# The feed-forward weights of a fused attention and FP4 feed-forward layer, begun a chunk in every second step

## What is computed

```python
q = elu(x @ Wq + bq) + 1; k = elu(x @ Wk + bk) + 1; v = x @ Wv + bv
k = k / sqrt(sum(k * k) + 1e-6)
out = (q @ k.T) @ v @ Wo + bo                 # by head
x = layernorm(x + (layernorm(x + out) * gamma + beta))

def fp4_quant_dequant(x):                      # of each block of 16
    scale = max(max(abs(xb)) / 6, 1e-12)
    q = GRID[searchsorted(MID, abs(xb / scale))] * sign(xb / scale) * scale
h = silu(fp4_linear(x, w_gate)) * fp4_linear(x, w_up)
x = layernorm(x + fp4_linear(h, w_down))
```

## Time and profile before

| | us |
|---|---|
| median of 3 runs | 755.93 (754.36 to 756.26) |
| the profiled execution | 755.5 |
| its span, first to last instruction | 753.7 |

### The profile page before, as it was taken

One profiled execution on the slowest core, in us unless ns is written; L12 is line 12 of the kernel. 1 busy time (PEld: TensorE's weight loads), 2 busy tenths in 40 slices (PEclk: granted clock), 3 DMA queues, 4 the chain that ended last, 5 costly groups with the idle time before them and its releaser, 6 DMA issues.

```text
span 753.7 us, 13645 instructions
## 1 busy us (share of the span) xinstructions
PE 703.5 (93%) x4162; PEld 623.6 (83%) x4162; DVE 584.1 (77%) x1433; ACT 479.0 (64%) x878; POOL 602.3 (80%) x891
## 2 busy tenths in 40 slices
PE   1979899999995699999999999999999999999996
PEld 0868678888884478999999999999999999999995
DVE  2678786565653588888888888888888888888775
ACT  2456566666663476767676776767676767767654
POOL 2488787787775899888888888888888888888766
PEclk9998999999998599999999999999999999999999
DMA  8232323443323110111112111211111111200001
GB/s 256 81 127 89 121 97 114 153 137 131 126 85 112 57 57 29 63 52 57 43 43 70 43 57 43 70 43 56 43 51 63 56 44 43 71 15 30 15 29 43
DMA packets 22188, 54.95 MB, mean 73 GB/s; under 512 B 2530, under 2 KB 5476, under 8 KB 22116
## 3 DMA queue, kind: packets, MB, share of 16 engines
q1 hardware_dynamic: 20992, 53.29, 20.5%
q10 hardware_dynamic: 1124, 0.79, 0.5%
HBM read 28.90 MB, written 25.17 MB: 72 GB/s over the span
## 4 chain that ended last, share of the span: by engine, by line
PE 79%; DVE 8%; issue 4%; POOL 3%; ACT 3%; DMA 2%; ACTq 0%; POOLq 0%; DVEq 0%; SPq 0%
PE banks L314 20%; PE banks L315 20%; PE banks L316 20%; PE banks L435 7%; PE banks L412 6%; PE banks L350 2%; DMA gamma_b<-in_L_attn_gamma_dram 1%; DVE arena L688 1%; PE banks L325 1%; DVE arena L701 1%; DVE arena L694 1%; ACT arena L511 1%; ACT arena L514 1%; DVE lnbuf L651 1%; DVE resid L667 1%
## 5 line engine op out<-in xcount | busy, mean ns | idle before, releaser
L314 PE MATMUL banks<-wgu_hi,actT_lo 128*128 128x512 f32 (+1 forms) x384 | 149.8, 390 | 1.6 <-DVE actT_lo L779 1.6
L315 PE MATMUL banks<-wgu_lo,actT_hi 128*128 128x512 f32 (+1 forms) x384 | 143.8, 374 | 0.0
L316 PE MATMUL banks<-wgu_hi,actT_hi 128*128 128x512 f32 (+1 forms) x384 | 142.9, 372 | 0.0
L314 PE MATMUL banks<-wd_hi,actT_lo 128*128 128x256 f32 x384 | 118.1, 308 | 0.0
L975 POOL TENSOR_TENSOR arena<-arena 128x960 f32<-128x960 f16 (+2 forms) x68 | 117.6, 1730 | 0.0
L583 ACT ACTIVATE arena<-banks 128x512 f32<-128x512 f32 x64 | 38.3, 598 | 124.3 <-PE banks L316 124.3
L955 POOL TENSOR_TENSOR arena<-arena 128x704 f32<-128x704 f32 x64 | 89.1, 1392 | 30.7 <-DVE arena L766 30.5
L316 PE MATMUL banks<-wd_hi,actT_hi 128*128 128x256 f32 x384 | 108.3, 282 | 0.0
L315 PE MATMUL banks<-wd_lo,actT_hi 128*128 128x256 f32 x384 | 108.3, 282 | 0.0
L779 DVE TENSOR_TENSOR actT_lo<-banks,actT_hi 128x512 fp32r<-128x512 f32 (+1 forms) x132 | 83.1, 668 | 16.3 <-ACT actT_hi L577 16.1
L412 PE MATMUL banks<-mo,resid 128*128 128x256 f32 x256 | 71.7, 405 | 13.1 <-DVE lnbuf L802 13.1
(11 more groups left out here) (114 smaller groups left out, 1862.2 us busy)
## 6 DMA issues: line engine op xcount, KB each, us to landing
x_plus_scratch<-xs SPq DMA_DIRECT2D x32, 512.0 KB, 2.9
xs<-x_plus_scratch SPq DMA_DIRECT2D x32, 512.0 KB, 3.3
arena<-in_L_attn_x_dram SPq DMA_DIRECT2D x32, 256.0 KB, 3.6
out_dram<-arena SPq DMA_DIRECT2D x32, 256.0 KB, 2.1
resid<-in_L_ffn_w_down_dram SPq DMA_DIRECT2D x1, 704.0 KB, 9.4
resid<-in_L_ffn_w_gate_dram SPq DMA_DIRECT2D x1, 640.0 KB, 9.0
resid<-in_L_ffn_w_up_dram SPq DMA_DIRECT2D x1, 640.0 KB, 10.2
resid<-in_L_attn_Wk_dram SPq DMA_DIRECT2D x1, 256.0 KB, 4.9
```

What stands on the lines that cost most here:

```text
L314: nc.tensor.matmul(dst, sl, mh, start=(k == 0 and not begun), stop=False, skip_group_check=shared)
L315: nc.tensor.matmul(dst, sh, ml, start=False, stop=False, skip_group_check=shared)
L316: last = nc.tensor.matmul(dst, sh, mh, start=False, stop=(k == n - 1), skip_group_check=shared)
```

## The change

A chunk is begun in every second step (`PACE = 2`): `w_scales` of chunk c in step 2c, `w_scaled_chunk` in 2c+1, `w_f16_chunk` in 2c+2, `w_round` and `w_deq_chunk` in 2c+3. `wy` and `wqn` become two rotating places of one chunk each, in a new piece of the arena, and two waits guard them: `w_f16_chunk(c)` waits for the dequantisation of chunk c-2, `w_scaled_chunk(c)` for the half-precision copy of c-2. `WG_STEP` is computed: a group comes in the first free step from 2 x (its last chunk) + 4 on, which gives 6, 7, 10, 11, 14, 16, 20, 21, 24 and 25. The staging places of the attention weights move to higher addresses of `resid`.

```diff
--- before.py
+++ after.py
@@ -110,6 +110,7 @@
         qe = take(2 * 512).rearrange("p (s n) -> p s n", s=2)
         ssq, se, seed = (take(64).rearrange("p (s n) -> p s n", s=2) for _ in range(3))
         klog, na, nb, ncb, knorm = (take(32) for _ in range(5))
+        w_words = take(3 * 384)
 
 
         at[0] = 0
@@ -129,9 +130,10 @@
         NW = 2 * I * D // P + D * I // P
         end = T * D
         wraw = scratch[:, end - NW:end]
-        wqn = scratch[:, end - NW - NW // 2:end - NW].bitcast(F16)
-        o = end - NW - NW // 2 - NW
-        wy = scratch[:, o:o + NW]
+        CW = 384
+        o = end - NW
+        wqn = w_words[:, 0:CW].bitcast(F16).rearrange("p (s n) -> p s n", s=2)
+        wy = w_words[:, CW:3 * CW].rearrange("p (s n) -> p s n", s=2)
         wkv_st = scratch[:, o - 1536:o - 512].rearrange("p (k n) -> p k n", k=KT)
         wq_st = scratch[:, o - 512:o].rearrange("p (k n) -> p k n", k=KT)
         NB = NW // BLK
@@ -199,7 +201,6 @@
 
         GU_TILES = 2 * I // P
         DW = KT * I
-        CW = 384
         NCH = NW // CW
         CH = [(c * CW, (c + 1) * CW) for c in range(NCH)]
         WG = []
@@ -211,7 +212,12 @@
             for k in range(KT):
                 cols = [DW + i * D + k * P for i in range(i0, i1)]
                 WG.append((cols, wgu_hi[:, k, i0 * P:i1 * P], wgu_lo[:, k, i0 * P:i1 * P]))
-        WG_STEP = {5 + g if g < 4 else 6 + g: g for g in range(len(WG))}
+
+        PACE = 2
+        WG_STEP = {}
+        for g, (cols, _, _) in enumerate(WG):
+            ready = PACE * ((max(cols) + P - 1) // CW) + 4
+            WG_STEP[max([ready] + [step + 1 for step in WG_STEP])] = g
 
         def wg_view(g):
             cols, hi, _ = WG[g]
@@ -220,6 +226,10 @@
 
         def wg_chunks(g):
             return (max(WG[g][0]) + P - 1) // CW + 1
+
+        def chunk_at(step):
+
+            return step // PACE if step % PACE == 0 and 0 <= step // PACE < NCH else None
 
         def there(t):
             return 0 <= t < T
@@ -490,7 +500,8 @@
             def w_f16_chunk(c):
                 a, b = CH[c]
                 act.wait_ge(w_scaled, c + 1)
-                nc.scalar.activation(wqn[:, a:b], halves(wy[:, a:b]), ACT.Copy, scale=F16_ONE).then_inc(w_f16, 1)
+                after(act, w_deq, c - 1)
+                nc.scalar.activation(wqn[:, c % 2, :], halves(wy[:, c % 2, :]), ACT.Copy, scale=F16_ONE).then_inc(w_f16, 1)
 
             def weights_high(g):
                 act.wait_ge(wT_ps, g + 1)
@@ -552,8 +563,8 @@
                     k_exps(p)
                 if p in WG_STEP:
                     weights_high(WG_STEP[p])
-                if 0 <= p - 2 < NCH:
-                    w_f16_chunk(p - 2)
+                if chunk_at(p - 2) is not None:
+                    w_f16_chunk(chunk_at(p - 2))
                 if pair(p):
                     k_squares(p)
 
@@ -663,7 +674,7 @@
 
             def w_round(c):
                 dve.wait_ge(w_f16, c + 1)
-                q = wqn[:, CH[c][0]:CH[c][1]].bitcast(U16)
+                q = wqn[:, c % 2, :].bitcast(U16)
                 nc.vector.tensor_scalar(q, q, ROUND_HALF, None, ALU.add).then_inc(w_half, 1)
                 dve.wait_ge(w_half, c + 1)
                 nc.vector.tensor_scalar(q, q, ROUND_MASK, None, ALU.bitwise_and).then_inc(w_rounded, 1)
@@ -731,10 +742,10 @@
                     v_bias(p)
                 if p in WG_STEP:
                     weights_low(WG_STEP[p])
-                if 0 <= p < NCH:
-                    w_scales(p)
-                if 0 <= p - 3 < NCH:
-                    w_round(p - 3)
+                if chunk_at(p) is not None:
+                    w_scales(chunk_at(p))
+                if chunk_at(p - 3) is not None:
+                    w_round(chunk_at(p - 3))
                 if pair(p):
                     k_sums(p)
 
@@ -881,14 +892,15 @@
             def w_scaled_chunk(c):
                 a, b = CH[c]
                 pool.wait_ge(w_scale_s, c + 1)
-                nc.gpsimd.tensor_tensor(blocks(wy[:, a:b]), blocks(wraw[:, a:b]), each(winv[:, a // BLK:b // BLK]),
+                after(pool, w_f16, c - 1)
+                nc.gpsimd.tensor_tensor(blocks(wy[:, c % 2, :]), blocks(wraw[:, a:b]), each(winv[:, a // BLK:b // BLK]),
                                         ALU.mult).then_inc(w_scaled, 1)
 
             def w_deq_chunk(c):
                 a, b = CH[c]
                 pool.wait_ge(w_rounded, c + 1)
                 pool.wait_ge(w_scaled, c + 1)
-                nc.gpsimd.tensor_tensor(blocks(wraw[:, a:b]), blocks(wqn[:, a:b]), each(ws14[:, a // BLK:b // BLK]),
+                nc.gpsimd.tensor_tensor(blocks(wraw[:, a:b]), blocks(wqn[:, c % 2, :]), each(ws14[:, a // BLK:b // BLK]),
                                         ALU.mult).then_inc(w_deq, 1)
 
             def k_newton(p):
@@ -927,10 +939,10 @@
                     pool.wait_ge(consts_in, 6 * 16)
                 if pair(p):
                     x_biases(p)
-                if 0 <= p - 1 < NCH:
-                    w_scaled_chunk(p - 1)
-                if 0 <= p - 3 < NCH:
-                    w_deq_chunk(p - 3)
+                if chunk_at(p - 1) is not None:
+                    w_scaled_chunk(chunk_at(p - 1))
+                if chunk_at(p - 3) is not None:
+                    w_deq_chunk(chunk_at(p - 3))
 
             def roots(t):
                 s = t % 2
```

## The result

The changed kernel takes 749.58 us (749.20 to 751.34) against 756.1 us of the kernel before, a ratio of 0.9921 with a 95% interval of 0.9906 to 0.9936: 6.0 us by the ratio, 6.5 by the medians. The forecast was 748.6 us, faster. The profiled execution of the changed kernel took 749.2 us for a span of 747.1.

The account below looks back on a forecast made before the run. The loop of ACT and DVE, lengthened by DVE instructions held by POOL, bounds loaded steps. Steps 2 to 21 at 128.3 us and 22 to 25 at 24.7 gain 7.3 us: median 748.6 us, range 742 to 756.5.

Parts of the forecast that it names:

- What bounds the loaded steps: Steps with weight work: the loop of ACT and DVE, not PE, sets the pace; some 14.3 us are stall.
- Odd steps: Steps 3 to 21, `w_round` held by POOL's two L919: nine at 6.3 us, step 21 at 7.1.
- Even steps without a group: Steps 2, 4, 8, 12, 18: 4.50 us fixed plus 1.65 for `w_scales`, 6.15 each.
- Even steps with a group: Steps 6, 10, 14, 16, 20: 6.15 us plus 0.60 for weights_low of 512 columns, 6.75 each.
- The sum: Steps 2 to 21 take 128.3 us, steps 22 to 25 24.7; step 26 begins 7.3 us earlier.
- the ring: Loop of ACT and DVE, one turn per step: 4.50 us fixed plus weight work, 7.64 in step 8 before.
- The new waits and places: Waits of ACT's copy and POOL's multiply for chunk c-2, and moved `wy` and `wqn`: costed at 0.
- Rival C: PE waits for POOL's dequantised chunk, some 0.7 us six times; 4 us of gain go, 751 to 753 us; chance 0.12.
- Rival B: PE sets the pace in the loaded steps, as locks are seldom met; 741 to 743 us; chance 0.14.
- D: Work only spread, every loaded step paying its own hold, 6.8 us a step; 754 to 758 us; chance 0.12.
- E: Slower: DVE held twice in each even and odd loaded step, from mean 6.9 us a step on; chance 0.10.
- The clock: PE's granted clock, 0.77 from 213 to 264 us, may shift: 2 us to either side, taken as 0.

Follow-up runs that it names:

- experiment 2: The changed kernel with DVE's `w_scales` and `w_round` both issued ahead of `q_features`; 742.95 us, ratio 0.9830.
- experiment 4: The changed kernel, DVE order kept, with each 512-column L931 of POOL cut into two of 256 columns; 745.94 us, ratio 0.9872.
- experiment 7: The changed kernel with `w_scales` and `w_round` ahead of `q_features` and each weight group one step later; 742.15 us, ratio 0.9815.
- experiment 1: The changed kernel with `PACE = 1`, a chunk in every step, rotating places and waits kept; 754.66 us, ratio 0.9987 to the kernel before.
- (3): The kernel before, a chunk in every step, with `w_round` and `w_scales` moved ahead of `q_features`; 746.25 us, ratio 0.9872.

## Why the prediction was right

- **What bounds the loaded steps.** Right. Moving DVE's calls (2) or shortening POOL's instructions (4) moves the time, and the most that could be gained, put at 13.9 to 14.3 us, is about what experiment 7 gains, 13.9.
- **Odd steps.** Right, by the place of L667 against POOL's two L919. Forecast 6.3; from one start of L513 to the next the changed kernel has 6.34 to 6.36 us in seven of the nine (5.92 in step 3, where L678 slips in ahead of the first L931; 6.66 in step 5), and 7.14 in step 21, forecast 7.1. The mean price of `w_round`, 5.58 a step, would have been wrong.
- **Even steps without a group.** Mis-sized: forecast 6.15 from the mean price of `w_scales`, measured 6.29 in step 2 and 6.50 to 6.52 in the other four, 1.6 us more in all. Here too the place decided: in steps 8, 12 and 18 L662 slips in ahead of the second L931 and L663 then is held for the whole of it; in step 4 the same happens a little earlier, with the first L931. Going by the rule of the Trainium skill (SBUF — State Buffer, section Who interferes with whom) the prediction had 6.6, the nearer value; the trace agrees with the page in that one of the two is held to the end of the second L931 in the eight even steps from 6 to 20. In step 4 it is held to the end of the first, in step 2 to that of L923.
- **Even steps with a group.** Forecast 6.75, measured 6.62 or 6.63 in all five, 0.6 us less in all: the weights_low of 0.60 is nearly swallowed, as L662 only meets the same end of POOL's instruction later. In step 10:

```profile
87.09 0.75 DVE L662 TENSOR_SCALAR lnbuf<-lnbuf 128x24 f32<-128x24 f32 x1
87.75 0.17 DVE L663 TENSOR_SCALAR lnbuf<-lnbuf 128x24 f32<-128x24 f32 x1
```

- **The sum.** 129.7 us for twenty rounds of the ring, forecast 128.3. Steps 22 to 25 took 25.44, forecast 24.7. So steps 2 to 25 gave 5.45 us where 7.3 were forecast; 0.47 us ahead of step 2 and 0.7 behind step 26, not forecast, brought the span to 6.6. That the median came out within 1 us of the forecast is in part luck: the steps missed by 1.85 us, and the two ends, which the forecast took as 0, gave 1.15 back.
- **The new waits and places** cost nothing to be seen: experiment 1 is 1 us under the kernel before, not over, with the two moved groups in it.
- **Rival C** named a real wait with the wrong size and count. It expected some 0.7 us in six steps; POOL's dequantisation delayed PE once, by 2.25 us in step 6, and the ring hid it: that step's ring took 6.62 us, as those of the other four with a group. It became a loss of its own only where the ring was short: 0.96 us in experiment 2, which experiment 7 removed, and 2.96 in experiment 4.
- **Rival B**, PE sets the pace, is not what the changed kernel does, but what it does once the calls stand elsewhere. **D** and **E** did not come: no even step went over 6.63 us.
- **The clock** behind step 30 gave little: 0.80 for 0.77 in the stretch from 213 to 264 us.

## What to carry to other kernels

Where one engine's small instructions take a multiple of their least duration, look up what the neighbour engine runs at that moment, and price them by their place in the step, not by their mean. Spreading such work over more steps gives its whole gain only where the sum of a few steps comes under the next bound. Moving it to where its engine waits anyway gained 9.8 us here by itself, though it was still held there (3), where spreading gained 6.5; it needs no memory and no new waits.

## What was not expected of the hardware

In all ten loaded even steps of the changed kernel only one of L662 and L663 was held, and it could be either: in step 8 the first took 0.18 us and the second 1.28, in step 10 the first 0.75 and the second 0.17. Less than 0.1 us can decide which. In the kernel before, L651 started at 31.07, 0.01 us ahead of an L919, and took 0.18 us, with 1.27 for L652; at 88.39 it started 0.06 behind an L919 and took 1.28, with 0.16 for L652. The sum was about the same. Two holds in a row occur too, as in step 8 before, where a shorter POOL instruction came next.

Cutting a POOL instruction of 512 columns in two made each half 744 ns instead of 1294, so POOL lost some 0.2 us on each pair, and the kernel gained 3.6 us all the same.

The first 28 us differ between profiled executions with nearly the same code there: step 2 started at 29.04, 28.57, 29.05, 29.02, 29.88 and 27.38 us in six kernels. With 2.5 us between the least and the greatest, a difference of that size between two spans should be read from the steps, not from the ends.
